# An FP8-rounded feed-forward block behind a long convolution on Trainium2: block 0's convolution pieces, one sum and three queue steps moved

## The chip, the cores and the metric

The kernel runs on one core of one Trainium2 chip. The metric is the device time of one execution in microseconds, as the median of several runs; a kernel's other numbers come from one execution that the hardware profiler recorded.

## What is computed

The input `x` is 128 x 32 x 512 float32: 128 samples, 32 channels, 512 positions. A state-space kernel of 512 taps per channel is computed from small parameters, every channel of `x` is convolved with its own taps (causally), a skip term `D` is added, positions behind a sample's length are set to zero, and the result goes through a gated feed-forward layer whose inputs are rounded to FP8 steps. Its output is added to `x`. Cut to what matters:

```python
def _L0_cond_ref(u, log_dt, C, log_A_real, A_imag, D, length):
    K = _get_kernel(log_dt, C, log_A_real, A_imag, Lq)
    ...
    y = jnp.fft.irfft(uf * kf[None], n=n)[..., :Lq]
    y = y + u * D[:, None]
    mask = (jnp.arange(Lq)[None, :] < length[:, None]).astype(u.dtype)
    return y * mask[:, None, :]

def _L0_ffn_ref(x, gate_w, up_w, down_w, ...):
    gate_out = _fake_quant_fp8_linear(x, gate_w, gate_in_scale, gate_w_scale)
    up_out = _fake_quant_fp8_linear(x, up_w, up_in_scale, up_w_scale)
    hidden = jax.nn.silu(gate_out) * up_out
    return _fake_quant_fp8_linear(hidden, down_w, down_in_scale, down_w_scale)

x = x + _L0_ffn_ref(_L0_cond_ref(x, ..., itok_B_78_3631), ...)
```

## The kernel before

**Tiles.** The 32 channels are cut into 8 blocks of 4; a block is 4 x 128 = 512 tokens. For each block the kernel does four things. TensorE convolves each channel `h` with a Toeplitz matrix of its taps (`conv`, matmuls `y_ps<-xt,toep`, float32, in four pieces called distances 0 to 3, of 512, 384, 256 and 128 columns). ScalarE and VectorE turn the result into rounded inputs `yq`. TensorE then multiplies them with the gate and up weights, in 11 chunks of the hidden size, each chunk 8 matmuls of 512 columns; ScalarE makes the SiLU (`sil<-gate_ps`), VectorE the product (`hv<-up_ps,sil`, function `product`) and the rounding of pairs of chunks (`hc` on ScalarE, `ht`, `hq` and a clip on VectorE). Last, TensorE multiplies `hq` with the down weights (`down_ps<-wd,hq`), ScalarE reads that out, and a DMA of the GpSimd queue adds it to `x` in `out`.

**The chain of one channel of y.** Convolution in `y_ps`; `mask_y` on VectorE (`ym<-y_ps,mask`); `scale_y` (`yv`, two activations) and `magnitude_y` (`yc`, two activations) on ScalarE; `sum_y` (`yt<-yc,yv`), `round_y` (`yq<-yc,yt`) and `clip_y` (`yq<-yq`) on VectorE.

**Order.** Every engine has its own instruction stream, written out by hand, with semaphores between them. A block is 11 slots, one for each chunk `c`. Beside chunk `c` of block `g`, TensorE does four down matmuls of block `g-1` and pieces of convolutions of later blocks, as the table `CONV_PLAN` says: an entry `c: [(step, h, distances)]` puts these pieces of channel `h` of block `g + step` into slot `c`. Channels 0 and most of 1 are done two blocks ahead, the rest one block ahead. VectorE's and ScalarE's work on y is placed by `MASK_PLAN`, `SCALE_PLAN`, `MAGNITUDE_PLAN`, `SUM_PLAN` and `ROUND_PLAN`. The gate matmuls of a chunk wait until the product of the chunk two before is done, since the two chunks share a PSUM bank:

```python
at_least(pe, silu_done, n - 1)
at_least(pe, prod_done, n - 1)
```

**Block 0** has nothing to run beside it yet, so it starts channel by channel: `by_channel(h)` does chunks 0 and 1 for channel `h` alone (128 columns, 16 matmuls), as soon as `clip_y(0, 0, h)` is done, with the convolutions of block 1's channels 0 and 1 between them. Slots 0 and 1 of block 0 then hold only convolution pieces, and slot 2 is the first with 512-column gate matmuls.

**Queues.** The SyncE queue (SP) stores the taps of the last 20 channels to a DRAM scratch when ScalarE has copied them from PSUM (`copy_k(2)`), and loads `xt` and `toep` of the next blocks and copies `x` to `out` (`copy_x`). `next_conv(3, 1)` waits for block 1's four convolutions (`y_ready` of 8), then loads block 3's `xt` and `toep`. The GpSimd queue loads the weights at the start.

In the trace, lines are: 489 `conv`, 515 `by_channel`, 547 gate and up, 503 down, 598 the last down part, 825 `mask_y`, 833 `sum_y`, 844 `round_y`, 851 `clip_y`, 860 `product`, 868, 877 and 885 the rounding of pairs, 362, 363, 370 and 373 `scale_y` and `magnitude_y`, 344 `copy_k`, 381 `hc`, 388 the read-out of down, 398 the SiLU.

Of the kernel before, what the change touches and what calls it, by code (L numbers as in the profile page):

```python
# [32 lines left out]
HB = 4  # L33
# [45 lines left out]
def adaln_ffn_kernel(nc, xT, xn, params, scales, unit, stepped, wg_d, wu_d, wd_d, out):  # L79
# [4 lines left out]
    with ExitStack() as ctx:  # L84
# [97 lines left out]
        def at_least(eng, s, v):  # L182

            if not (isinstance(v, int) and v <= 0):
                eng.wait_ge(s, v)

        def k_in_bank(i, half):

            js = K_GROUPS[i]
            bank, lo = (down_ps, gate_ps, down_ps)[i][half], (0, 0, 2 * KB)[i]  # L190
            return bank[0:KA, lo:lo + (js.stop - js.start) * KB].rearrange("p (j b) -> p j b", b=KB)

        def rows_of_k(i, half):
            return krow[:].rearrange("p (j f) b -> p j f b", f=2)[:, K_GROUPS[i], half]
# [18 lines left out]
        def _(sp):  # L213
# [8 lines left out]
            def load_x_t(g, par):  # L222
                sp.dma_start(xt[par][:], xT[g]).then_inc(xt_in[par], 16)

            def load_toep(g, par):
                sp.dma_start(toep[par][:], toep_d[g]).then_inc(conv_in[par], 16)

            def copy_x(g, par):
                sp.dma_start(out[:, bass.ts(g, HB), :], xn[:, bass.ts(g, HB), :]).then_inc(copied[par], 16)
# [25 lines left out]
            def next_conv(g, par):  # L255
                at_least(sp, y_ready, HB * (g - 1))
                load_x_t(g, par)
                load_toep(g, par)
# [2 lines left out]
            load_x_t(2, 0)  # L261
            sp.wait_ge(k_stored[2], 16)
            load_toep(2, 0)
            copy_x(0, 0)
            next_conv(3, 1)
            copy_x(1, 1)
            with sp.Fori(0, (NBLK - 4) // 2) as j:
                for par in range(2):
# [49 lines left out]
        def _(act):  # L318
# [21 lines left out]
            def copy_k(i):  # L340

                for half in range(2):
                    act.wait_ge(k_ready, 2 * i + half + 1)
                    nc.scalar.copy(rows_of_k(i, half), k_in_bank(i, half)).then_inc(k_copied, 1)
# [67 lines left out]

            act.wait_ge(scales_ready, 1)
            for h in range(HB):
                if h:
                    scale_y(0, h)
                else:
                    cols = slice(0, L // 2)
                    act.wait_ge(ym_first, 1)
                    nc.scalar.activation(yv[0][:, 0, cols], ym[0][:, cols], ACT.Copy,  # L420
                                         scale=fac[:, D_GATE:D_GATE + 1]).then_inc(yv_first, 1)
                    nc.scalar.activation(yv[0][:, 1, cols], ym[0][:, cols], ACT.Copy,
                                         scale=fac[:, D_UP:D_UP + 1]).then_inc(yv_first, 1)
                    act.wait_ge(ym_done, 1)
                magnitude_y(0, h)
            copy_k(2)
            scale_y(1, 0)
            magnitude_y(1, 0)
            slots(0, 0, None, True, 2)
# [10 lines left out]
        def _(pe):  # L440
# [67 lines left out]
            def by_channel(h):  # L508

                pe.wait_ge(yq_ready, h + 1)  # L510
                cols = slice(h * B, (h + 1) * B)
                for c in range(2):
                    for ps, wt, version, ready in ((gate_ps, wg, 0, gate_ready), (up_ps, wu, 1, up_ready)):
                        for k in range(LB):
                            mm = nc.tensor.matmul(ps[c][:, cols], wt[:, k, c * P:(c + 1) * P],
                                                  yq[0][:, version, k, cols], start=(k == 0), stop=(k == LB - 1))
                        if h == HB - 1:
                            mm.then_inc(ready, 1)

            def beside(g, par, half, c, down, ahead):  # L520

                for step, h, distances in CONV_PLAN.get(c, ()):
                    if step <= ahead and (down or (step, h) != (1, 1)):
                        conv(g + step, (par + step) % 2, half + (1 if step == 2 else par), h, distances)
                if down:
                    down_part(g - 1, 1 - par, c)
# [44 lines left out]
            by_channel(1)  # L571
            conv(1, 1, 0, 1, [0, 1, 3, 2])
            by_channel(2)
            by_channel(3)
            pe.wait_ge(middle_in, 32)
            slots(0, 0, 0, False, 2)
# [28 lines left out]
        def _(dve):  # L605
# [222 lines left out]
            def sum_y(g, h):  # L828

                m = HB * g + h  # L830
                q = h % 2
                at_least(dve, yscaled, m + 1)
                v.scalar_tensor_tensor(yt[q][:], yc[q][:], FLOOR, yv[q][:], ALU.max, ALU.add).then_inc(yt_done, 1)  # L833
# [75 lines left out]
            def slots(g, par, ahead, before, plan):  # L909
                first = before is None  # L910
                for c in range(CH):
# [16 lines left out]
                    if c in plan and c < 9 and not (first and c == 3):  # L928
                        rounded(PAIRS * g + plan[c], g, par, plan[c])
                    if ahead and c in SUM_PLAN and not (first and c == 2):  # L930
                        sum_y(g + 1, SUM_PLAN[c])
                    if c - 1 in plan:
# [70 lines left out]

CONV_PLAN = {
# [5 lines left out]
MASK_PLAN = {0: 1, 3: 2, 5: 3}  # L1012
SCALE_PLAN = {0: (1, 0), 1: (1, 1), 4: (1, 2), 6: (1, 3)}
MAGNITUDE_PLAN = {1: (1, 0), 2: (1, 1), 5: (1, 2), 7: (1, 3)}
SUM_PLAN = {2: 0, 3: 1, 6: 2, 8: 3}
ROUND_PLAN = {4: 0, 5: 1, 7: 2, 9: 3}
H_BEHIND = {3: 0, 7: 1, 10: 2}
H_EVEN = {3: 0, 7: 1, 9: 2, 10: 3}
# [60 lines left out]
```

## Time and profile before

| what | us |
|---|---|
| median of 3 runs (325.42 to 325.95) | 325.68 |
| the profiled execution's own time | 325.52 |
| its span, first to last instruction | 323.8 |
| TensorE busy (PE) | 310.2 (96%) |
| VectorE busy (DVE) | 303.2 (94%) |
| ScalarE busy (ACT) | 206.9 (64%) |

The profiled time is 1.72 us longer than the span. The granted TensorE clock is 1.000 of 2.4 GHz in all of it. A line of the timeline is: start in us, duration in us, engine, line of the kernel, operation, output and inputs with shape, count of merged instructions, and in brackets how long the engine sat idle before it and what ended that. TensorE's matmuls are pipelined and their ends are modelled, so a row's duration reaches over the start of the next one: the pace of TensorE is read from one start to the next, and its real gap can be larger than the idle time in the bracket. Some matmul records are missing: a group of four then shows as three.

### The profile page before, as it was taken

The page shows a single profiled execution, that of the slowest core. Times are in us where ns is not written, and L with a number is a line of the kernel's source. Part 1 is how long each engine was busy: PE and PEld are TensorE (multiplying, and loading weights), DVE is VectorE, ACT ScalarE, POOL GpSimd, SP SyncE. Part 2 cuts the span into 40 slices and gives each one's busy share as a digit, 9 for nine tenths or more (in the row PEclk, how much of TensorE's full clock was granted, in tenths as well). Part 3 has the DMA queues.
Part 4 walks back from the last instruction along what each step waited for, and adds up shares of the span by engine and source line. Part 5 has one row for each costly group of instructions (what it writes and reads, how often), then busy time and mean ns, then how long its engine had stood idle before and what let it go on. Part 6 is the DMA issues. An engine that isn't in the chain of part 4 may idle for free.

```text
span 323.8 us, 4771 instructions
## 1 busy us (share of the span) xinstructions
PE 310.2 (96%) x1569; PEld 162.9 (50%) x1595; DVE 303.2 (94%) x464; ACT 206.9 (64%) x318; POOL 12.5 (4%) x20
## 2 busy tenths in 40 slices
PE   1999999999999999999999999999999999989996
PEld 1467554545455554555455454555455454534444
DVE  6999999999999999999998999989998999989784
ACT  4858788188755777486845868376863959364540
POOL 2031000000001000010001000010001000010010
PEclk9999999999999999999999999999999999999999
DMA  6879999300002690078202780067401650051028
GB/s 201 181 181 231 268 278 383 148 1 2 0 0 28 150 343 3 1 130 279 110 0 36 165 317 1 0 121 249 150 0 16 134 243 0 0 97 34 2 31 228
DMA packets 14014, 38.38 MB, mean 119 GB/s; under 512 B 1470, under 2 KB 6558, under 8 KB 11052
## 3 DMA queue, kind: packets, MB, share of 16 engines
q1 hardware_dynamic: 8412, 26.58, 23.2%
q0 software_dynamic: 5584, 11.57, 20.6%
q8 instruction: 10, 0.16, 0.2%
q14 instruction: 8, 0.07, 0.1%
HBM read 33.90 MB, written 15.81 MB: 154 GB/s over the span
## 4 chain that ended last, share of the span: by engine, by line
PE 72%; DVE 19%; issue 4%; ACT 4%; DMA 1%; DVEq 0%; ACTq 0%
PE gate_ps L547 19%; PE up_ps L547 18%; PE down_ps L503 17%; PE y_ps L489 15%; DVE hv L860 3%; DVE yq L844 3%; DVE yt L833 2%; DVE hq L877 2%; DVE ht L868 2%; PE y_ps L598 1%; DVE ym L825 1%; PE down_ps L598 1%; ACT hc L381 1%; DMA prm<-in_params 1%; DVE hq L885 1%
## 5 line engine op out<-in xcount | busy, mean ns | idle before, releaser
L398 ACT ACTIVATE sil<-gate_ps,fac 128x512 f32<-128x512 f32 (+1 forms) x88 | 59.6, 680 | 67.8 <-PE gate_ps L547 66.8
L547 PE MATMUL gate_ps<-yq,wg 128*128 128x512 bf16 (+3 forms) x365 | 88.2, 363 | 2.7 <-DVE hv L860 2.4
L547 PE MATMUL up_ps<-yq,wu 128*128 128x512 bf16 (+3 forms) x367 | 88.4, 363 | 0.3
L489 PE MATMUL y_ps<-xt,toep 128*128 128x512 f32 (+1 forms) x248 | 78.1, 434 | 0.0
L503 PE MATMUL down_ps<-wd,hq 128*128 128x512 bf16 (+1 forms) x295 | 76.8, 379 | 0.7
L860 DVE SCALAR_TENSOR_TENSOR hv<-up_ps,fac,sil 128x512 f32<-128x512 f32 (+1 forms) x88 | 65.5, 744 | 8.2 <-ACT sil L398 6.6
L381 ACT ACTIVATE hc<-hv 128x1024 f32<-128x1024 f32 (+1 forms) x48 | 47.0, 980 | 20.9 <-DVE hq L877 19.8
L547 PEld LDWEIGHTS gate_ps<-yq,wg 128*128 128x128 bf16 x372 | 35.6, 100 | 43.6 <-ACT sil L398 4.0
L489 PEld LDWEIGHTS y_ps<-xt,toep 128*128 128x128 f32 x248 | 45.9, 190 | 19.9 <-issue 2.4
L868 DVE SCALAR_TENSOR_TENSOR ht<-hc,hv 128x1024 f32<-128x1024 f32 (+1 forms) x48 | 54.1, 1127 | 1.9 <-ACT hc L381 1.9
L547 PEld LDWEIGHTS up_ps<-yq,wu 128*128 128x128 bf16 x372 | 36.3, 100 | 38.3
L877 DVE SCALAR_TENSOR_TENSOR hq<-hc,ht 128x1024 bf16<-128x1024 f32 (+1 forms) x48 | 53.8, 1126 | 0.3
L503 PEld LDWEIGHTS down_ps<-wd,hq 128*128 128x128 bf16 (+1 forms) x308 | 30.1, 98 | 37.9 <-issue 12.6
L844 DVE SCALAR_TENSOR_TENSOR yq<-yc,yt 128x1024 bf16<-128x1024 f32 x32 | 39.0, 1217 | 0.1
L833 DVE SCALAR_TENSOR_TENSOR yt<-yc,yv 128x1024 f32<-128x1024 f32 x31 | 37.7, 1217 | 0.0
L370 ACT ACTIVATE yc<-ym,fac 128x512 f32<-128x512 f32 x32 | 22.8, 713 | 2.9 <-DVE yq L844 2.9
L362 ACT ACTIVATE yv<-ym,fac 128x512 f32<-128x512 f32 x31 | 22.1, 712 | 3.2 <-DVE ym L825 3.2
L373 ACT ACTIVATE yc<-ym,fac 128x512 f32<-128x512 f32 x32 | 22.8, 712 | 0.0
L363 ACT ACTIVATE yv<-ym,fac 128x512 f32<-128x512 f32 x31 | 22.0, 709 | 0.0
L825 DVE TENSOR_TENSOR ym<-y_ps,mask 128x512 f32<-128x512 f32 x31 | 21.1, 681 | 0.0
L388 ACT ACTIVATE res<-down_ps,fac 128x512 f32<-128x512 f32 x28 | 19.0, 679 | 2.2 <-PE down_ps L503 2.1
L885 DVE TENSOR_SCALAR hq<-hq 128x1024 bf16<-128x1024 bf16 (+1 forms) x48 | 18.4, 397 | 0.3
(155 smaller groups left out, 118.1 us busy)
## 6 DMA issues: line engine op xcount, KB each, us to landing
xt<-in_xT SPq DMA_DIRECT2D x8, 1024.0 KB, 7.6
out<-in_x SPq DMA_DIRECT2D x7, 1024.0 KB, 5.6
out<-res POOLq DMA_DIRECT2D x7, 1024.0 KB, 7.8
toep<-kpad_scratch SPq DMA_DIRECT2D x6, 1024.0 KB, 10.0
toep<-kpad_scratch SPq DMA_DIRECT2D x8, 256.0 KB, 3.9
wd<-in_down POOLq DMA_DIRECT2D x1, 1280.0 KB, 21.3
xt<-in_x SPq DMA_DIRECT2D x1, 1024.0 KB, 7.3
out<-xt SPq DMA_DIRECT2D x3, 256.0 KB, 3.1
```

The source lines that it names most:

```text
L370: gate = nc.scalar.activation(yc[q][:, 0, :], ym[q][:], ACT.Abs, scale=fac[:, R_GATE:R_GATE + 1])
L381: nc.scalar.activation(hc[e % 2][0:w, 0:k], hv[e % 2][0:w, 0:k], ACT.Abs, scale=UP20).then_inc(abs_ready, 1)
L398: nc.scalar.activation(sil[b][0:w, :], gate_ps[b][0:w, :], ACT.Silu, scale=fac[0:w, S_GATE:S_GATE + 1]).then_inc(silu_done, 1)
L489: last = nc.tensor.matmul(y_ps[h % 2][:, d * P:L], toep[par][:, h, d * P:(d + 1) * P], xt[par][:, h, 0:L - d * P], start=(d == 0), stop=(d ...
L503: mm = nc.tensor.matmul(down_ps[t % 2][:], hq[par][0:w, k, t * P:(t + 1) * P], wd[0:w, k, :], start=(k == 0), stop=(k == CH - 1))
L547: mm = nc.tensor.matmul(ps[b][0:w, cols], wt[:, k, c * P:c * P + w], yq[par][:, version, k, cols], start=(k == 0), stop=(k == LB - 1))
L825: v.tensor_tensor(ym[q][:], y_ps[q][:], mask[:].rearrange("p k b -> p (k b)"), ALU.mult).then_inc(ym_done, 1)
L833: v.scalar_tensor_tensor(yt[q][:], yc[q][:], FLOOR, yv[q][:], ALU.max, ALU.add).then_inc(yt_done, 1)
L844: v.scalar_tensor_tensor(yq_of(par, h), yc[q][:].rearrange("p v (k b) -> p (v k) b", k=LB), FLOOR, yt[q][:].rearrange("p v (k b) -> p (v k ...
L860: v.scalar_tensor_tensor(hv[c // 2 % 2][0:w, c % 2], up_ps[b][0:w, :], fac[0:w, S_UP:S_UP + 1], sil[b][0:w, :], ALU.mult, ALU.mult).then_i ...
L868: v.scalar_tensor_tensor(ht[e % 2][0:w, 0:k], hc[e % 2][0:w, 0:k], FLOOR, hv[e % 2][0:w, 0:k], ALU.max, ALU.add).then_inc(t_done, 1)
L877: v.scalar_tensor_tensor(hq[par][0:w, 2 * e:2 * e + k, :], hc[e % 2][0:w, 0:k], FLOOR, ht[e % 2][0:w, 0:k], ALU.max, ALU.subtract, reverse ...
```

## The change

Five edits:

1. In front of `by_channel(3)`, TensorE does the first piece (distance 0, 512 columns) of channel 2 of block 1.
2. In block 0 a table of its own, `FIRST_PLAN`, takes the place of `CONV_PLAN`; every piece there comes one slot earlier.
3. `SUM_PLAN` has 9 in place of 8 for channel 3, in all blocks that have a block behind them: `sum_y` of the fourth channel comes behind the product of chunk 9 (the tenth) and right in front of its own `round_y`.
4. `copy_k(2)` on ScalarE comes ahead of `scale_y(0, 3)` in place of behind `magnitude_y(0, 3)`.
5. On the SyncE queue `next_conv(3, 1)` comes ahead of `copy_x(0, 0)`.

```diff
@@ -261,8 +261,8 @@
             load_toep(2, 0)
+            next_conv(3, 1)
             copy_x(0, 0)
-            next_conv(3, 1)
             copy_x(1, 1)
@@ -412,6 +412,8 @@
             for h in range(HB):
+                if h == HB - 1:
+                    copy_k(2)
                 if h:
                     scale_y(0, h)
@@ -423,7 +425,6 @@
                 magnitude_y(0, h)
-            copy_k(2)
             scale_y(1, 0)
@@ -519,8 +520,8 @@
-                for step, h, distances in CONV_PLAN.get(c, ()):
-                    if step <= ahead and (down or (step, h) != (1, 1)):
+                for step, h, distances in (CONV_PLAN if down else FIRST_PLAN).get(c, ()):
+                    if step <= ahead:
@@ -571,6 +572,7 @@
             by_channel(2)
+            conv(1, 1, 0, 2, [0])
             by_channel(3)
@@ -1003,6 +1005,10 @@
+FIRST_PLAN = {
+    6: [(2, 0, [0])], 7: [(2, 0, [1, 3])], 8: [(2, 0, [2]), (2, 1, [0])], 9: [(2, 1, [1, 3])],
+    1: [(1, 2, [1, 3])], 2: [(1, 2, [2]), (1, 3, [0])], 3: [(1, 3, [1, 3])], 4: [(1, 3, [2])],
+}
 CONV_PLAN = {
     7: [(2, 0, [0])], 8: [(2, 0, [1, 3])], 9: [(2, 0, [2]), (2, 1, [0])], 10: [(2, 1, [1, 3])],
@@ -1012,7 +1018,7 @@
-SUM_PLAN = {2: 0, 3: 1, 6: 2, 8: 3}
+SUM_PLAN = {2: 0, 3: 1, 6: 2, 9: 3}
```

**TensorE, from the end of the third channel's `by_channel` to slot 3 of block 0.** Before:

```order
L515 MATMUL up_ps<-yq,wu 128x128 x4
L515 MATMUL gate_ps<-yq,wg 128x128 x4
L515 MATMUL up_ps<-yq,wu 128x128 x4
L515 MATMUL gate_ps<-yq,wg 128x128 x4
L515 MATMUL up_ps<-yq,wu 128x128 x4
L489 MATMUL y_ps<-xt,toep 128x512
L547 MATMUL gate_ps<-yq,wg 128x512 x4
L547 MATMUL up_ps<-yq,wu 128x512 x4
L489 MATMUL y_ps<-xt,toep 128x384
L489 MATMUL y_ps<-xt,toep 128x128
```

and now:

```order
L516 MATMUL up_ps<-yq,wu 128x128 x4
L490 MATMUL y_ps<-xt,toep 128x512
L516 MATMUL gate_ps<-yq,wg 128x128 x4
L516 MATMUL up_ps<-yq,wu 128x128 x4
L516 MATMUL gate_ps<-yq,wg 128x128 x4
L516 MATMUL up_ps<-yq,wu 128x128 x4
L490 MATMUL y_ps<-xt,toep 128x384
L490 MATMUL y_ps<-xt,toep 128x128
L548 MATMUL gate_ps<-yq,wg 128x512 x4
L548 MATMUL up_ps<-yq,wu 128x512 x4
```

The 512-column piece went from behind the fourth channel's 16 matmuls to ahead of them, and the 384 and 128 columns from behind the first 512-column chunk to ahead of it.

**VectorE, slots 8 to 10 of block 0** (a number behind a name is the buffer; `hv` is the product, `yt` the sum, `yq` the rounding and then the clip). Before:

```order
L860 SCALAR_TENSOR_TENSOR hv0<-up_ps0,fac,sil0 128x512
L868 SCALAR_TENSOR_TENSOR ht1<-hc1,hv1 128x1024
L833 SCALAR_TENSOR_TENSOR yt1<-yc1,yv1 128x1024
L885 TENSOR_SCALAR hq0<-hq0 128x1024
L860 SCALAR_TENSOR_TENSOR hv0<-up_ps1,fac,sil1 128x512
L844 SCALAR_TENSOR_TENSOR yq1<-yc1,yt1 128x8x128
L851 TENSOR_SCALAR yq1<-yq1 128x8x128
L860 SCALAR_TENSOR_TENSOR hv1<-up_ps0,fac,sil0 96x512
```

and now:

```order
L862 SCALAR_TENSOR_TENSOR hv0<-up_ps0,fac,sil0 128x512
L870 SCALAR_TENSOR_TENSOR ht1<-hc1,hv1 128x1024
L887 TENSOR_SCALAR hq0<-hq0 128x1024
L862 SCALAR_TENSOR_TENSOR hv0<-up_ps1,fac,sil1 128x512
L835 SCALAR_TENSOR_TENSOR yt1<-yc1,yv1 128x1024
L846 SCALAR_TENSOR_TENSOR yq1<-yc1,yt1 128x8x128
L853 TENSOR_SCALAR yq1<-yq1 128x8x128
L862 SCALAR_TENSOR_TENSOR hv1<-up_ps0,fac,sil0 96x512
```

The sum `yt1` left the place two ahead of the tenth product and now stands directly in front of the rounding that reads it; the number of instructions is the same.

## Rows read from the trace of the kernel before

**Rows 1.** Busy time by stretch: slots 2 to 10 of block 0, block 1, block 2.
```profile
core 0: us, PE busy (x) PEld busy (x) DVE busy (x) ACT busy (x) POOL busy (x), PEclk, DMA share, GB/s
...
36.80:61.40 24.60, 23.62 (x100) 12.18 (x100) 24.43 (x31) 17.34 (x26) 0.00 (x0) 1.00 1.02 317
61.40:98.94 37.54, 37.27 (x168) 19.10 (x173) 36.90 (x48) 24.08 (x36) 0.00 (x0) 1.00 0.00 1
98.94:136.09 37.15, 36.99 (x170) 19.30 (x172) 36.61 (x48) 25.39 (x38) 0.90 (x1) 1.00 0.40 114
```
**Rows 2.** Timeline of TensorE around the fourth channel and slot 2 of block 0.
```profile
34.93 0.39 PE L515 MATMUL up_ps<-yq,wu 128*128 128x128 bf16 x4
35.59 0.40 PE L515 MATMUL gate_ps<-yq,wg 128*128 128x128 bf16 x4 [0.27 <-DVE yq L851]
...
36.49 1.08 PE L489 MATMUL y_ps<-xt,toep 128*128 128x512 f32 x2
37.93 0.81 PE L547 MATMUL gate_ps<-yq,wg 128*128 128x512 bf16 x3 [0.36 <-DVE hv L860]
```
**Rows 3.** Timeline of VectorE, the same stretch, then slots 8 to 10.
```profile
35.45 1.22 DVE L833 SCALAR_TENSOR_TENSOR yt<-yc,yv 128x1024 f32<-128x1024 f32 x1
36.82 0.75 DVE L860 SCALAR_TENSOR_TENSOR hv<-up_ps,fac,sil 128x512 f32<-128x512 f32 x1
...
58.97 1.22 DVE L833 SCALAR_TENSOR_TENSOR yt<-yc,yv 128x1024 f32<-128x1024 f32 x1
60.11 0.42 DVE L885 TENSOR_SCALAR hq<-hq 128x1024 bf16<-128x1024 bf16 x1
60.45 0.74 DVE L860 SCALAR_TENSOR_TENSOR hv<-up_ps,fac,sil 128x512 f32<-128x512 f32 x1
61.11 1.21 DVE L844 SCALAR_TENSOR_TENSOR yq<-yc,yt 128x1024 bf16<-128x1024 f32 x1
```
**Rows 4.** Timeline of TensorE, first gate matmuls of slots 0, 2, 3, 7, block 1.
```profile
61.43 0.82 PE L547 MATMUL gate_ps<-yq,wg 128*128 128x384 bf16 x4 [0.60 <-DVE hv L860]
...
68.03 1.02 PE L547 MATMUL gate_ps<-yq,wg 128*128 128x512 bf16 x4
...
71.55 1.02 PE L547 MATMUL gate_ps<-yq,wg 128*128 128x512 bf16 x4
...
84.70 1.02 PE L547 MATMUL gate_ps<-yq,wg 128*128 128x512 bf16 x4
```
**Rows 5.** Timeline of VectorE, products of block 1 that those gates wait for.
```profile
67.13 0.75 DVE L860 SCALAR_TENSOR_TENSOR hv<-up_ps,fac,sil 128x512 f32<-128x512 f32 x1
...
70.66 0.75 DVE L860 SCALAR_TENSOR_TENSOR hv<-up_ps,fac,sil 128x512 f32<-128x512 f32 x1
...
83.80 0.75 DVE L860 SCALAR_TENSOR_TENSOR hv<-up_ps,fac,sil 128x512 f32<-128x512 f32 x1
```
**Rows 6.** Timeline of VectorE, one sum followed by its own rounding.
```profile
29.14 1.22 DVE L833 SCALAR_TENSOR_TENSOR yt<-yc,yv 128x1024 f32<-128x1024 f32 x1
30.39 1.23 DVE L844 SCALAR_TENSOR_TENSOR yq<-yc,yt 128x1024 bf16<-128x1024 f32 x1
```
**Rows 7.** Timelines of VectorE and TensorE, blocks 6 and 7, the stretch's first and last.
```profile
264.10 1.23 DVE L868 SCALAR_TENSOR_TENSOR ht<-hc,hv 128x1024 f32<-128x1024 f32 x1
...
292.20 0.74 DVE L860 SCALAR_TENSOR_TENSOR hv<-up_ps,fac,sil 128x512 f32<-128x512 f32 x1
...
293.08 1.02 PE L547 MATMUL gate_ps<-yq,wg 128*128 128x512 bf16 x4 [0.22 <-DVE hv L860]
```
**Rows 8.** Timeline of ScalarE around `copy_k(2)`.
```profile
28.92 0.72 ACT L362 ACTIVATE yv<-ym,fac 128x512 f32<-128x512 f32 x1 [0.77 <-DVE ym L825]
...
31.39 0.71 ACT L344 COPY hq<-down_ps 16x320 f32<-16x320 f32 x2
```
**Rows 9.** DMA issues: block 2's Toeplitz load at 39.36; the small down-weight load.
```profile
toep<-kpad_scratch SPq DMA_DIRECT2D x1, 1024.0 KB, 9.8
...
wd<-in_down POOLq DMA_DIRECT2D x1, 96.0 KB, 26.2
```

## The prediction, written before the changed kernel ran

> **What bounds the kernel now.** I read the busy time by stretch first. From slot 2 of block 0 to the end of block 1 both TensorE and VectorE are nearly full: VectorE 24.43 of 24.60 us in block 0 and 36.90 of 37.54 in block 1, TensorE 23.62 and 37.27 [rows 1]. From block 2 on TensorE needs 37.15 us a block, with 36.99 busy, and the same 37.15 returns in blocks 3 to 5, so TensorE is the bound there. Block 1 is 0.39 us longer than block 2 for the same work. So the question is which of the two engines is late at the end of block 0, and that needs the timelines.
>
> A gate group of TensorE starts right behind the product of the chunk two before, where that product is late. The product of chunk 0 of block 1 starts at 67.13 and takes 0.75, the gate of slot 2 starts at 68.03, 0.15 behind its end; the products at 70.66 and 83.80 stand the same way to the gates at 71.55 and 84.70 [rows 4, 5]. So TensorE follows VectorE up to 84.70 us, and the idle times of 0.27, 0.36 and 0.60 us before it in block 0 [rows 2, 4] are what it has in hand over VectorE. VectorE meanwhile works back to back: from its first product at 36.82 [rows 3] to 65.1 us its timeline has no idle row, then one of 0.26 us, which is a loop through VectorE's own results (its rounding lets ScalarE make `hc`, which lets VectorE go on). A delay of VectorE at 36.8 us is therefore carried to 84.70, and TensorE, full from there, to the end.
>
> **The change, part by part.**
>
> *The first piece ahead of the fourth channel.* TensorE ends the third channel at about 35.15 (four starts of 0.056 us from 34.93) and waits until 35.59 for the fourth channel's `yq` [rows 2], a gap of 0.44 us by starts. The piece is 512 columns in float32: its two records are followed by the next work 0.86 us after the first in every slot where TensorE doesn't wait. It fills the 0.44 and pushes the fourth channel back by 0.42: to 36.01. Behind that channel hang the first SiLU and the first product of VectorE. VectorE is ready for it: the sum before it starts at 35.45 and the next instruction could follow 1.13 us later, at 36.58, yet the product starts at 36.82 [rows 3], when the SiLU is there. So the product goes to 37.24, and **VectorE loses 0.42 us**. The bounds: nothing, if the product waited for something else; 0.50 if the change of float32 to bf16 matmuls costs a little more. I take 0.42.
>
> *The rest of the pieces one slot earlier.* This is 0.86 us of TensorE work taken from behind slot 2's gate and put ahead of it, where TensorE waits for the product anyway (before, idle 0.36 at 37.93 [rows 2]). The total is unchanged. With it TensorE runs from slot 2 at 38.1 to slot 10, which ends at about 60.2 (22.96 us before, less 0.86). That leaves it 0.5 to 0.9 us ahead of each product. Cost nothing, gain nothing, since VectorE is the one that is late. If VectorE weren't full, this would be worth the gap of 0.44.
>
> *The fourth sum behind the tenth product.* In block 0 the tenth product now comes one sum earlier: from 60.45 back by 1.14 (58.97 to 60.11 [rows 3]) and on by the 0.42, to 59.73. The gate of block 1's slot 0, which waits 0.60 us for it [rows 4], can start at about 60.7 instead of 61.43. But the stall doesn't vanish, it moves. The sum and its rounding now follow each other: such a pair is 1.25 us apart [rows 6], against 1.14 for a sum followed by an instruction that doesn't read it [rows 3]. So **VectorE loses 0.11 us more**, the fourth `yq` is ready at 63.3, where TensorE now asks for it, and the product of chunk 0 of block 1 moves from 67.13 by 0.42 + 0.11 to 67.66. The gate at 68.03 then starts at 68.56. What is late next is that product: TensorE comes a good 1 us too early for it and waits.
>
> A rule speaks against this 0.11. The Trainium skill (VectorE: DVE Perf Modes, The DRAIN you can't avoid) says that the next VectorE instruction can't start until the pipeline is empty and that a semaphore between two costs nothing extra. By it the term would be 0 and the sum 0.42. The rows show 1.25 against 1.14, and I go by them.
>
> *In blocks 1 to 5* the same pair costs 0.11 in VectorE each time, but VectorE has slack there (36.61 busy of 37.15 in block 2 [rows 1]; from block 2 on it waits 0.6 to 1.3 us a block for a SiLU in slot 0): nothing. *In block 6* it is different: TensorE has less to do beside it, and VectorE runs back to back from 264.10, with one idle of 0.72 that again is the loop through its own roundings, to the product at 292.20, which the gate at 293.08 waits for [rows 7]. So the last 0.11 us count once more. Bounds 0 and 0.12.
>
> *`copy_k(2)` earlier.* Its two copies are 0.71 us and come into an idle 0.77 of ScalarE that ends at 28.92 [rows 8]. Their sources are ready at about 28.1, so `scale_y(0, 3)` is late by 0.1 at most; its result is used by VectorE only at 32.59, 1.1 us after it is there. Nothing. On the SyncE queue the store and the loads of block 2's `xt` and `toep` come up to 3.2 us earlier.
>
> *`next_conv(3, 1)` ahead of `copy_x(0, 0)`.* Block 1's last convolution ends at about 45.9, so block 3's loads go out 2 us earlier and `copy_x(0, 0)` 6 us later than 39.8. The copy is wanted by ScalarE only at block 1's slot 5 (some 77 us). Block 2's Toeplitz load took 9.8 us from 39.36 [rows 9], to 49.2; its first piece was due at 51.52 and is now due at 49.4. Issued at 36 to 39 with no copy beside it, it lands in time. The cover is thin only if none of the 3.2 us comes through.
>
> **The sum.** 0.42 + 0.11 + 0.11 = 0.64 us. The profiled execution took 325.52, so 326.16 by it; the median of the runs is 0.16 above the profiled one, and I add to the median: 325.68 + 0.65 = **326.3**.
>
> **The rivals.**
>
> *Faster: TensorE is the real bound.* If VectorE has slack that the timeline hides, the three idle times of TensorE, 0.27 + 0.36 + 0.60 = 1.23 us [rows 2, 4], are what can be won, and the time is 324.5. For it speaks that TensorE has the highest busy share. Against it, the three gates of block 1 at exactly 0.15 us behind their products. It decides if the product at 67.13 comes earlier than now. The Trainium skill (Perfetto Trace Analysis, Optimization Strategies) would have it so: keep the matmul engine as highly used as possible. Chance 0.13.
>
> *No change: the delay of the first product is smaller or partly absorbed.* The product waits 0.24 us now; if part of the 0.42 hides in waits that I read as back to back, 0.0 to 0.3 us are left, 325.9. Chance 0.20.
>
> *Slower by more: a transfer becomes late.* If block 2's Toeplitz load lands where it did, 49.2, or up to 1.5 us later because `xt` and the weights share the engines with it, or if the small down-weight load (31.3 + 26.2 = 57.5 [rows 9]), wanted at 60.7, is pushed back by more than 4 us, TensorE stalls until VectorE runs dry: 1 us on top of the sum, 327.3. Chance 0.07.
>
> *The change doesn't do what it says* for the queue steps: the store lands when it did, since the DMA engines are full; this costs nothing and changes no number.
>
> The forecast itself has 0.60.
>
> **How the numbers follow.** Two tenths of a per cent, 0.65 us, is about what a measurement of this kernel can tell from no change, and the forecast sits on that line: I give 0.33 of its 0.60 to slower and 0.27 to the same. Slower is 0.33 + 0.07 = 0.40, the same 0.27 + 0.20 = 0.47, faster 0.13. The range reaches from 325.1, below the unchanged case, to 327.0, the forecast with both bounds and the runs' spread; outside are most of the faster case and most of the late transfer.
>
> **What would show it.** Right: the fourth channel's first gate at 36.0, the first product at 37.2; the gate of block 1 at about 60.7, with no long wait; then a wait before the gate of slot 2, which starts near 68.6; block 2 starting near 99.5 (98.94 before); sum to rounding 1.25 apart in every block. Wrong: the first product still at 36.8, or block 2 starting at or below 98.9, or an idle row of TensorE in front of a `y_ps` piece at 49 us.

## The result and the profile after

The changed kernel takes 326.39 us (median of 17 runs, 326.12 to 327.55), the kernel before 325.61 us beside it (17 runs, 325.42 to 326.16). The ratio is 1.0027, 95% interval 1.0021 to 1.0034, so it is slower by more than 0.2%. The profiled execution took 326.39 against 325.52, its span 324.7 against 323.8, with the granted clock at 1.000 of 2.4 GHz again. TensorE's busy time is unchanged at 310.2 us; VectorE's is 303.8 in place of 303.2.

Line numbers of the kernels below are 0 to 10 above those of before, by the lines added. The busy time by stretch of the changed kernel, with the stretches moved by about their shift (+0.6 at slot 2, +0.74 at block 2), answers to [rows 1]:

```profile
core 0: us, PE busy (x) PEld busy (x) DVE busy (x) ACT busy (x) POOL busy (x), PEclk, DMA share, GB/s
37.40:62.00 24.60, 23.88 (x105) 12.58 (x106) 24.37 (x31) 17.27 (x26) 0.00 (x0) 1.00 1.00 296
61.60:99.68 38.08, 36.91 (x165) 18.52 (x168) 37.38 (x49) 24.10 (x36) 0.00 (x0) 1.00 0.00 1
99.68:136.83 37.15, 36.99 (x170) 19.30 (x172) 36.58 (x47) 25.05 (x38) 0.90 (x1) 1.00 0.40 114
```

VectorE is as full as before, and TensorE idles 1.17 of 38.08 us in the second stretch, where it idled 0.27 of 37.54 before: it got ahead and waits. Block 2 takes 37.15 us again.

TensorE's timeline, which answers to [rows 2, 4, 7]:

```profile
35.32 1.08 PE L490 MATMUL y_ps<-xt,toep 128*128 128x512 f32 x2
36.24 0.39 PE L516 MATMUL gate_ps<-yq,wg 128*128 128x128 bf16 x4
...
37.13 1.08 PE L490 MATMUL y_ps<-xt,toep 128*128 128x384 f32 x4
38.56 0.81 PE L548 MATMUL gate_ps<-yq,wg 128*128 128x512 bf16 x3 [0.34 <-DVE hv L862]
...
60.91 0.82 PE L548 MATMUL gate_ps<-yq,wg 128*128 128x384 bf16 x4 [0.33 <-DVE hv L862]
...
68.76 1.02 PE L548 MATMUL gate_ps<-yq,wg 128*128 128x512 bf16 x4 [0.81 <-DVE hv L862]
...
85.44 1.02 PE L548 MATMUL gate_ps<-yq,wg 128*128 128x512 bf16 x4
...
293.95 1.02 PE L548 MATMUL gate_ps<-yq,wg 128*128 128x512 bf16 x4 [0.22 <-DVE hv L862]
```

Block 1 starts 0.52 us earlier than before (61.43, now 60.91), and all of it is given back before slot 2's gate, most of it in a wait of 0.81 us that was not there. From there to block 6 every gate is 0.74 us late (68.03 to 68.76 is 0.73, 84.70 to 85.44), and at block 7 0.87 (293.08 to 293.95).

VectorE's timeline, which answers to [rows 3, 5]:

```profile
35.60 1.22 DVE L835 SCALAR_TENSOR_TENSOR yt<-yc,yv 128x1024 f32<-128x1024 f32 x1
37.45 0.75 DVE L862 SCALAR_TENSOR_TENSOR hv<-up_ps,fac,sil 128x512 f32<-128x512 f32 x1 [0.63 <-ACT sil L398]
...
59.93 0.74 DVE L862 SCALAR_TENSOR_TENSOR hv<-up_ps,fac,sil 128x512 f32<-128x512 f32 x1
60.59 1.21 DVE L835 SCALAR_TENSOR_TENSOR yt<-yc,yv 128x1024 f32<-128x1024 f32 x1
61.84 1.23 DVE L846 SCALAR_TENSOR_TENSOR yq<-yc,yt 128x1024 bf16<-128x1024 f32 x1
63.10 0.43 DVE L853 TENSOR_SCALAR yq<-yq 128x1024 bf16<-128x1024 bf16 x1
...
67.87 0.75 DVE L862 SCALAR_TENSOR_TENSOR hv<-up_ps,fac,sil 128x512 f32<-128x512 f32 x1
```

Before, the product came 1.37 us behind the sum (35.45, 36.82), now 1.85 (35.60, 37.45): 0.48 us lost. The tenth product is at 59.93, which is 60.45 - 1.14 + 0.63, the shift that it started with and one sum less. Sum and rounding are 1.25 apart (60.59, 61.84), rounding and clip 1.26 (61.84, 63.10). The product of chunk 0 of block 1 is 0.74 late. So the 0.87 of the profiled executions is:

| part | us | read from |
|---|---|---|
| all of the start is late | 0.15 | sum of the fourth channel, 35.45 to 35.60 |
| first product, behind that sum | 0.48 | 1.37 to 1.85 |
| sum in front of its own rounding, block 0 | 0.11 | 0.74 at 67.87, less 0.63 at 37.45 |
| the same, block 6 | 0.13 | 0.87 at 293.95, less 0.74 |

The first row is in none of the edits. Block 0's first convolution starts 0.17 us later than before, when its Toeplitz load has landed (issued at 14.36 before and 14.30 now, ahead of everything that the edits move), and VectorE's fourth sum comes 17.68 and 17.66 us behind that start. The start in the kernel before and in the changed one:

```profile
17.77 0.92 PE L560 MATMUL y_ps<-xt,toep 128*128 128x256 f32 x4
```

```profile
17.94 0.92 PE L561 MATMUL y_ps<-xt,toep 128*128 128x256 f32 x4 [0.35 <-DMA toep<-kpad_scratch]
```

### The profile page after: what moved, and what is told of

It is laid out like the page before. It is cut to its first block, busy times and chain, and to the rows that moved or that the text cites. A ratio compares the mean times of both kernels' runs of the same rounds, so it can differ in the third digit from the quotient of the medians.

```text
span 324.7 us, 4771 instructions
## 1 busy us (share of the span) xinstructions
PE 310.2 (96%) x1569; PEld 162.5 (50%) x1595; DVE 303.8 (94%) x464; ACT 206.6 (64%) x318; POOL 12.5 (4%) x20
## 4 chain that ended last, share of the span: by engine, by line
PE 76%; DVE 16%; issue 4%; DMA 2%; ACT 1%; DVEq 0%; ACTq 0%; SPq 0%
PE y_ps L490 19%; PE gate_ps L548 18%; PE up_ps L548 17%; PE down_ps L504 17%; DVE hv L862 3%; DVE yq L846 3%; DVE hq L879 2%; DVE ht L870 2%; DVE yt L835 2%; PE y_ps L600 1%; DMA toep<-kpad_scratch 1%; PE down_ps L600 1%; ACT hc L381 1%; DVE hq L887 1%; DMA prm<-in_params 1%
```

## The experiments

Each ran in 5 rounds against the kernel before, whose median was 325.64, 325.55, 325.62 and 325.61 in the four groups of runs (e1 to e4; e5 to e8; e9, e10; e11, e12). Theory A is the account that the prediction gives, with the first term as measured. A rival stands with its letter in the expectation that names it.

### e1: the pieces alone

```diff
+            conv(1, 1, 0, 2, [0])
             by_channel(3)
-                for step, h, distances in CONV_PLAN.get(c, ()):
+                for step, h, distances in (CONV_PLAN if down else FIRST_PLAN).get(c, ()):
```

> The kernel before with edits 1 and 2 alone: the piece ahead of the fourth channel and the table FIRST_PLAN. Theory A (VectorE's chain sets the time from block 0 to 84.7 us, and the piece delays its first product): the first product of VectorE starts 1.85 us behind the sum before it (1.37 in the kernel before), block 2 starts 0.48 us later, the time is 0.48 us longer (ratio 1.0015). Theory B (TensorE's gaps are what counts, and the loss comes from the moved sum or the queues): the gap of 0.44 us is filled, the time is 0 to 0.44 us shorter (ratio 0.9987 to 1.0000).

Measured: 326.04 us, ratio 1.0014 (1.0005 to 1.0023). Its VectorE and TensorE timelines:

```profile
35.49 1.22 DVE L834 SCALAR_TENSOR_TENSOR yt<-yc,yv 128x1024 f32<-128x1024 f32 x1
37.14 0.75 DVE L861 SCALAR_TENSOR_TENSOR hv<-up_ps,fac,sil 128x512 f32<-128x512 f32 x1 [0.43 <-ACT sil L398]
```

```profile
35.01 1.08 PE L489 MATMUL y_ps<-xt,toep 128*128 128x512 f32 x2
35.92 0.39 PE L515 MATMUL gate_ps<-yq,wg 128*128 128x128 bf16 x4
...
61.75 0.82 PE L547 MATMUL gate_ps<-yq,wg 128*128 128x384 bf16 x4 [1.46 <-DVE hv L861]
```

The product comes 1.65 behind its sum, so 0.28 is lost and not 0.48. The piece explains it: it starts where the third channel ends, at 35.01 here and at 35.32 in the changed kernel, and the product follows the piece by 2.13 us in both (37.14, 37.45). The loss is the end of the third channel plus 2.13, against the sum plus 1.37; TensorE was 0.31 earlier in this execution and VectorE 0.11, and the difference of 0.20 is that between the two losses. The term depends on how the engines happen to stand to each other, and that is set at the first convolution: it starts at 17.94 in the changed kernel and at 17.62 here, TensorE's piece is 17.4 us behind it in both, but the sum is 17.66 behind it there and 17.87 here. In all six executions where that convolution started at 17.77 or later, the sum came 17.66 to 17.68 behind it; where it started earlier, VectorE did not follow in full (17.71 us and more). The other half of the account holds too: without the moved sum, TensorE waits 1.46 us at block 1's first gate, its lead of one slot and no gain.

### e2: the sum alone

```diff
-SUM_PLAN = {2: 0, 3: 1, 6: 2, 8: 3}
+SUM_PLAN = {2: 0, 3: 1, 6: 2, 9: 3}
```

> The kernel before with edit 3 alone: the fourth sum behind the tenth product in all blocks. Theory A: the gate of block 1 no longer waits (it starts at 60.7 in place of 61.4, idle 0), but the gate of slot 2 of block 1 starts 0.12 us later (68.15), block 2 too (99.06), and a second 0.12 comes in at block 7 (the gate that was at 293.08 comes at 293.32); the time is 0.24 us longer (ratio 1.0007). Theory B: the stall of 0.60 us that goes away is a gain, the time is up to 0.6 us shorter (ratio 0.9982).

Measured: 325.97 us, ratio 1.0017 (1.0008 to 1.0026). Its VectorE and TensorE timelines:

```profile
60.19 1.22 DVE L833 SCALAR_TENSOR_TENSOR yt<-yc,yv 128x1024 f32<-128x1024 f32 x1
61.44 1.23 DVE L844 SCALAR_TENSOR_TENSOR yq<-yc,yt 128x1024 bf16<-128x1024 f32 x1
```

```profile
60.89 0.81 PE L547 MATMUL gate_ps<-yq,wg 128*128 128x384 bf16 x4
...
68.36 1.02 PE L547 MATMUL gate_ps<-yq,wg 128*128 128x512 bf16 x4 [0.81 <-DVE hv L860]
```

The wait of 0.60 ahead of block 1 [rows 4] is gone and stands at slot 2 with 0.81 us: the stall moved and grew. That gate is 0.33 later than before, of which 0.21 is the start (fourth sum at 35.66 where it was 35.45), so 0.12 belongs to the pair, and another 0.12 to 0.14 is in the gate at 293.55, behind block 6. These executions show that the start moves by itself: nothing that the fourth sum waits for is changed in e1, e2 and e5 to e8, and it stood at 35.49, 35.66, 35.46, 35.42, 35.40 and 35.70 (in e8 the clip ahead of it alone took 0.69 us, in the kernel before 0.43).

### e3: the queue steps alone

```diff
+            next_conv(3, 1)
             copy_x(0, 0)
-            next_conv(3, 1)
+                if h == HB - 1:
+                    copy_k(2)
-            copy_k(2)
```

> The kernel before with edits 4 and 5 alone: the tap copies and their store sooner, block 3's loads ahead of the first copy of x. Theory A: no time in it, ratio 1.0000 within 0.0003. The store on the SyncE queue goes out 3 us sooner (29 in place of 32), the Toeplitz load 2 to 3 us sooner. Theory C (the part of the loss that the VectorE chain does not explain, some 0.15 us that the changed kernel's timeline already shows at 34 us, comes from ScalarE's new order or the transfers): 0.15 us longer, ratio 1.0005, and the clip of the fourth channel starts at 35.26 in place of 35.10.

Measured: 325.56 us, ratio 1.0001 (0.9992 to 1.0009). The fourth sum is at 35.45 and block 2 starts at 98.95 (before 35.45 and 98.94): the queue steps cost nothing, and theory C falls: the 0.15 us do not come from them. The ScalarE timeline, which answers to [rows 8]:

```profile
28.06 0.73 ACT L344 COPY hq<-down_ps 16x320 f32<-16x320 f32 x2
28.93 0.72 ACT L362 ACTIVATE yv<-ym,fac 128x512 f32<-128x512 f32 x1
```

The copies fit into the idle time, and the scale step starts at 28.93 where it was 28.92. (In the changed kernel it starts at 29.09, but there the mask step that it reads is 0.17 us later too, by the start.) One thing is new in this profile, though: block 2 takes 37.44 us (98.95 to 136.39). Its TensorE timeline, SyncE timeline and DMA issues:

```profile
122.72 1.03 PE L548 MATMUL up_ps<-yq,wu 128*128 128x512 bf16 x4
123.77 1.12 PE L490 MATMUL y_ps<-xt,toep 128*128 128x512 f32 x2
```

```profile
112.50 0.41 SPq L226 DMA_DIRECT2D toep<-kpad_scratch  x1
```

```profile
toep<-kpad_scratch SPq DMA_DIRECT2D x1, 1024.0 KB, 11.0
```

The first piece of block 4 is due 0.86 behind the up matmuls, at 123.58, and starts at 123.77; its Toeplitz load was issued at 112.50 and took 11.0 us, to 123.5. This load had hardly any time in hand; the row does not name what the piece waited for. e11 tests it.

### e4: the 512 columns back behind the fourth channel

```diff
@@ the changed kernel
-            conv(1, 1, 0, 2, [0])
             by_channel(3)
-    1: [(1, 2, [1, 3])], 2: [(1, 2, [2]), (1, 3, [0])], ...
+    0: [(1, 2, [0])], 1: [(1, 2, [1, 3])], 2: [(1, 2, [2]), (1, 3, [0])], ...
```

> The changed kernel with edit 1 undone: the 512-column piece stands behind the fourth channel again, so that slots 0 and 1 of block 0 do the pieces of 512, 384 and 128 columns in a row, all else as changed. Theory A: the first product is on time again (1.37 us behind the sum before it), and 0.48 us come back: 0.24 us longer than the kernel before (ratio 1.0007), 0.5 to 0.6 shorter than the changed kernel. TensorE reaches slot 2 at about 37.8 and starts there 0.1 to 0.2 us later than before, at most 0.1 us of which could reach the time. Theory B: the time stays at that of the changed kernel, 0.88 us longer.

Measured: 326.24 us, ratio 1.0023 (1.0011 to 1.0036). **This missed**: the product is on time again and the time hardly came back. VectorE's, TensorE's and ScalarE's timelines:

```profile
35.61 1.22 DVE L834 SCALAR_TENSOR_TENSOR yt<-yc,yv 128x1024 f32<-128x1024 f32 x1
36.98 0.75 DVE L861 SCALAR_TENSOR_TENSOR hv<-up_ps,fac,sil 128x512 f32<-128x512 f32 x1
...
48.57 0.75 DVE L861 SCALAR_TENSOR_TENSOR hv<-up_ps,fac,sil 128x512 f32<-128x512 f32 x1 [0.23 <-ACT sil L398]
...
67.82 0.75 DVE L861 SCALAR_TENSOR_TENSOR hv<-up_ps,fac,sil 128x512 f32<-128x512 f32 x1
```

```profile
36.66 1.94 PE L490 MATMUL y_ps<-xt,toep 128*128 128x512 f32 x6
38.65 0.81 PE L548 MATMUL gate_ps<-yq,wg 128*128 128x512 bf16 x3
```

```profile
45.11 0.69 ACT L398 ACTIVATE sil<-gate_ps,fac 128x512 f32<-128x512 f32 x1 [1.91 <-PE gate_ps L548]
...
47.87 0.67 ACT L398 ACTIVATE sil<-gate_ps,fac 128x512 f32<-128x512 f32 x1
```

The product is 1.37 behind its sum. But now both slots' pieces stand between the fourth channel and slot 2, and its gate starts at 38.65, 0.72 later than before (37.93) where the start moved by 0.16. TensorE is then late for the next slots, ScalarE's SiLU starts at 45.11 and the one after it, behind its other work, at 47.87 (before 44.38 and 47.14), and VectorE's product waits for that at 48.57. The product of block 1 is 0.69 late. Of the 0.69, 0.16 is the start and 0.11 the pair of the moved sum, so 0.42 came this way. As these rows read, TensorE has in block 0 only the 0.36 us ahead of slot 2 [rows 2] in hand over the products, less than a piece, and what exceeds it comes back through ScalarE. The pieces one slot earlier are free in the changed kernel only because the first of them went ahead of the fourth channel, and there it costs 0.48. This way of the 0.42 is read from one trace; no run has the pieces in this order without the moved sum.

### e5 and e6: the sum moved in blocks 1 to 5, and in block 6

```diff
@@ the kernel before, with sums in place of SUM_PLAN
+                    sums = {2: 0, 3: 1, 6: 2, 9 if 0 < g < 6 else 8: 3}
```

e6 has `9 if g == 6 else 8` there.

> The kernel before with the fourth sum behind the tenth product in blocks 1 to 5 alone. Theory A (the pair of a sum and its own rounding costs VectorE 0.12 us, and that reaches the time only where VectorE is the late engine): VectorE shows 1.25 us from sum to rounding in these five blocks, its wait for a SiLU in slot 0 gets shorter by the same, blocks 2 to 6 start when they did (98.94, 136.09, 173.24, 210.39, 247.54, behind a shift of up to 0.2 of the start), and the time is unchanged, ratio 1.0000. Theory D (each such pair costs its 0.12 us wherever it stands): five times 0.12, 0.6 us longer, ratio 1.0018.

> The kernel before with the fourth sum behind the tenth product in block 6 alone. Theory A: everything up to block 7 is unchanged, the last gate of block 7 that waits for VectorE (293.08) comes 0.12 us later, the time is 0.12 us longer, ratio 1.0004, which the clock alone can hardly tell from 1; the trace decides. If VectorE had slack there: no shift at all.

Measured: e5 325.80 us, ratio 1.0005 (0.9996 to 1.0013); e6 325.69, ratio 1.0006 (0.9997 to 1.0016). Medians can't tell 0.1 us from nothing here, but the traces can. In e5 the blocks start at 98.96, 136.11, 173.26, 210.41 and 247.56, 37.15 apart to the hundredth, block 7's gate is at 293.10 where it was 293.08 [rows 7], and its execution took 325.54: the pair is hidden in the middle blocks, and the 1.0018 of theory D lies outside the interval. In e6 the start was 0.03 early, sum and rounding of block 6 are 1.25 apart (279.10, 280.35), and that gate is at 293.18: 0.13 net. As the prediction had it.

### e7: each clip of y behind the next product

```diff
@@ the kernel before
                     product(n, m, par, c)
+                    if ahead and c - 1 in ROUND_PLAN and not (first and c == 5):
+                        clip_y(g + 1, 1 - par, ROUND_PLAN[c - 1])
                         round_y(g + 1, 1 - par, ROUND_PLAN[c])
-                        clip_y(g + 1, 1 - par, ROUND_PLAN[c])
```

The change made a dependent pair; this takes one apart. The clip reads what the rounding just wrote; here a product stands between them.

> The kernel before, with the clip of each y moved from right behind its rounding to behind the next product, in all blocks: the same instructions, but no clip follows the rounding that it reads. Theory A says that this gives VectorE 0.11 us a pair: 3 pairs in block 0 and 1 in block 1 before the product at 83.8, and 4 in block 6. So block 2 starts 0.44 us sooner (98.50), and a second 0.44 us comes before the gate that was at 293.08; the time is 0.8 to 0.9 us shorter, ratio 0.9973 to 0.9976. Theory E, that two dependent instructions cost VectorE nothing extra: the time is unchanged; the clip of the fourth y comes 0.7 us later, and if TensorE waits for it, 0.1 us longer. The Trainium skill (VectorE: DVE Perf Modes, The DRAIN you can't avoid) states what theory E says: a semaphore between two VectorE instructions costs nothing extra.

Measured: 324.86 us, ratio 0.9977 (0.9969 to 0.9986), the first kernel here that is clearly faster. Its VectorE timeline, TensorE timeline and waits of VectorE (us in total, times, longest):

```profile
60.81 1.21 DVE L844 SCALAR_TENSOR_TENSOR yq<-yc,yt 128x1024 bf16<-128x1024 f32 x1
61.94 0.74 DVE L860 SCALAR_TENSOR_TENSOR hv<-up_ps,fac,sil 96x512 f32<-96x512 f32 x1
62.60 0.41 DVE L851 TENSOR_SCALAR yq<-yq 128x1024 bf16<-128x1024 bf16 x1
...
269.24 0.75 DVE L860 SCALAR_TENSOR_TENSOR hv<-up_ps,fac,sil 128x512 f32<-128x512 f32 x1 [0.19 <-ACT sil L398]
```

```profile
61.13 0.82 PE L547 MATMUL gate_ps<-yq,wg 128*128 128x384 bf16 x4 [0.44 <-DVE hv L860]
...
67.63 1.03 PE L547 MATMUL gate_ps<-yq,wg 128*128 128x512 bf16 x4
```

```profile
DVE hv L860 <- ACT sil L398: 8.8, 15, 1.0
```

From the rounding to what follows it is 1.13 us (60.81, 61.94), against 1.26 from a rounding to its own clip, shown above for the changed kernel. Slot 2's gate comes at 67.63 for 68.03, block 2 at 98.33 for 98.94. From the first product to that of chunk 0 of block 1, with three pairs taken apart between, it is 29.94 us (36.76, 66.70) for 30.31: 0.12 a pair. A dependent pair costs 0.11 to 0.13 us of VectorE, and where VectorE is the late engine, that is time.

The total is a little less than was expected, 0.69 us by the medians, and it is not spread as was expected. Block 2 is 0.56 us early net of the start (0.05), in place of 0.44: the product that the gate at 84.70 waited for passes its clip too (it is 0.87 us earlier, 82.93 for 83.80), and TensorE no longer waits there. The gate that was at 293.08 comes at 292.39, only 0.08 more: in block 6 VectorE now waits for a SiLU at 269.24, where it ran back to back, so most of what it saves there goes into that wait. Over the whole execution it waits 8.8 us for SiLUs, in 15 places, before 6.6 in 7. Part of e7's gain is thus the product's new place and not the pairs; the 0.12 above is free of that.

In this kernel every instruction that reads the one ahead also waits for the semaphore that the one ahead raises, so no run tells whether the read or that wait costs the 0.12. The rule of the Trainium skill (VectorE: DVE Perf Modes, The DRAIN you can't avoid), by which the pair would have cost nothing extra, does not hold for these pairs (1.26 against 1.13 us); the measurement decides.

### e8: and in slot 1 the sum ahead of the clips

```diff
@@ e7, slot 1
-                    clip(last - 2, 1 - par, PAIRS - 3)
-                    clip(last - 1, 1 - par, PAIRS - 2)
                     rounded_sum(last, PAIRS - 1)
+                    clip(last - 2, 1 - par, PAIRS - 3)
                     rounded(last, g - 1, 1 - par, PAIRS - 1)
+                    clip(last - 1, 1 - par, PAIRS - 2)
                     clip(last, 1 - par, PAIRS - 1)
```

> As the run before it, and in slot 1 of every block the five instructions on the last pairs (two clips, then a sum, a rounding and a clip that each read the one before) are put in the order sum, clip, rounding, clip, clip. Theory A: the sum-rounding and rounding-clip stalls of this short chain (0.05 and 0.06 us) go, 0.1 us at block 1 and 0.1 us at block 7; 0.2 us shorter than the run before it, ratio 0.9967 to 0.9970. Theory E: no difference. If TensorE has become the late engine by then, as it may where its own work is back to back, less than 0.2 us.

Measured: 324.72 us, ratio 0.9971 (0.9960 to 0.9982), the lowest of all, but no clear gain over e7, whose interval it overlaps, and less than the 0.2 us that were expected. In its profile nothing is won at block 2 (98.62, with the fourth sum at 35.70; 0.57 early net of the start, e7 0.56); the gate behind block 6 is at 292.44, 0.89 early net of the start, e7 0.64. It beats the kernel before by 0.8 to 0.9 us and the changed one by 1.7.

### e9: the changed kernel with e7's clips

> The changed kernel with the clips moved as in the run of the clips (each clip of y behind the next product). Theory A: the delays and the savings of VectorE in block 0 simply add, so the first product is again 1.85 us behind the sum before it, and block 2 starts 0.55 to 0.6 us sooner than in the changed kernel, which is where the kernel before has it, within 0.1 us (98.9 to 99.2, behind a shift of the start of up to 0.3); the time is 0.7 to 0.9 us shorter than the changed kernel's, ratio to the kernel before 0.9998 to 1.0006. If the piece ahead of the fourth channel had been hidden by a faster VectorE after all, the time would be that of the clips alone, ratio 0.9977.

The edit is that of e7, made to the changed kernel. Measured: 325.71 us, ratio 0.9996 (0.9987 to 1.0005), a hair below what was expected. In its profile the first product is 1.84 behind the sum (35.46, 37.30) as in the changed kernel, and block 2 starts at 98.98 for 99.68, which is 0.56 us net of the start. The gain and the loss add up, since both are VectorE's. Block 2 again takes 0.40 too much (98.98 to 136.53), with the same piece late.

### e10: only half of the piece ahead

```diff
@@ the kernel before: 256 columns of the 512, the other 256 behind the fourth channel
+            half_piece(0)
             by_channel(3)
```

If the full piece costs because it is larger than the gap of 0.44 us, half of it should fit.

> The kernel before, with only half of the 512-column piece (256 columns, 0.43 us of TensorE) ahead of the fourth channel, the other half where the whole piece stood; FIRST_PLAN and the other edits are not in it. Theory A (what counts is how far the piece sticks out of the gap of 0.44 us): the half fits, the first product stays 1.37 us behind the sum (at most 1.43), nothing after it moves, and the time is unchanged, ratio 1.0000 within 0.0004. If what costs is that anything at all stands between the third and the fourth channel (a change of operand type, another weight load), the product is late by 0.1 us or more and the time follows it, ratio 1.0003 or more. If TensorE's earlier arrival at slot 2 were worth something, ratio below 0.999.

Measured: 325.53 us, ratio 0.9999 (0.9990 to 1.0008). Its TensorE and VectorE timelines:

```profile
34.99 0.65 PE L525 MATMUL y_ps<-xt,toep 128*128 128x256 f32 x2
35.50 0.40 PE L515 MATMUL gate_ps<-yq,wg 128*128 128x128 bf16 x4
...
37.84 0.81 PE L556 MATMUL gate_ps<-yq,wg 128*128 128x512 bf16 x3 [0.78 <-DVE hv L870]
```

```profile
35.36 1.22 DVE L843 SCALAR_TENSOR_TENSOR yt<-yc,yv 128x1024 f32<-128x1024 f32 x1
36.73 0.75 DVE L870 SCALAR_TENSOR_TENSOR hv<-up_ps,fac,sil 128x512 f32<-128x512 f32 x1
```

It fits: 1.37 behind the sum, nothing lost, although work of another type stands between the two channels. And nothing is won: TensorE's wait for the product, 0.36 before, is 0.78. Work put into a gap of an engine that isn't late makes its next gap longer.

### e11 and e12: the Toeplitz loads ahead of the copy in the SyncE loop

```diff
@@ e3, and e8 for e12
+                    next_conv(2 * j + 4 + par, par)
                     at_least(sp, added[par], 16 * (j + 1))
                     copy_x(2 * j + 2 + par, par)
-                    next_conv(2 * j + 4 + par, par)
```

> The queue edits (4 and 5) plus one more in the SyncE loop: the loads of xt and toep of block g + 4 go ahead of the wait for the sum of block g and of copy_x, so block 4's Toeplitz load, which lands 0 to 1.6 us before its first piece needs it, should be issued near 82 us and not at 112. Theory F (a load that comes just in time caused the one-off of 0.3 and 0.4 us in block 2 of two profiled executions): block 2 takes 37.15 in this profile, the piece near 123.6 starts without delay; the median is that of the kernel before or up to 0.1 us less, ratio 0.9990 to 1.0005. Rival G (a disturbance of another kind, not the load): the one-off has no tie to the load, and comes or not as before. Rival H (the earlier loads now run beside other transfers): a wait elsewhere, 0.2 us or more slower.

> The fastest kernel so far (the clips of y behind the next product, and in slot 1 the sum ahead of the two clips; 324.72 us) with the same step in the SyncE loop. The kernel of the later clips issued the block 4 load at 111.39, landed 121.7 and used it at 123.24: 1.5 us in hand. Theory F: nothing to win in the median, ratio to the kernel before 0.9965 to 0.9975. Rival H: above 0.9980.

Measured: e11 325.66 us, ratio 1.0003 (0.9994 to 1.0012); e12 324.74, ratio 0.9968 (0.9958 to 0.9978), no better than e8. The SyncE and TensorE timelines of e11:

```profile
81.91 0.39 SPq L226 DMA_DIRECT2D toep<-kpad_scratch  x1
```

```profile
123.55 1.02 PE L490 MATMUL y_ps<-xt,toep 128*128 128x512 f32 x2
```

The load is issued 30 us earlier, the piece is on time, and block 2 takes 37.15 (98.92 to 136.07). In the profiled executions of the other ten experiments and both kernels the load was issued between 111.32 and 113.02 (111.87 before, 113.02 after), and took 9.9 to 11.5 us. In e3 it landed at 123.50 with its piece due at 123.58, in e9 at 123.7 (112.20 + 11.5) with the piece due at 123.61, and these two pieces were 0.2 and 0.3 late; in all the others it landed 0.4 us or more ahead, e10 with 11.1 us from 111.96 among them, and no piece was late. That fits a load just in time (theory F). H, that the earlier load hurts elsewhere, is excluded by e12, whose interval ends below the 0.9980 set for it; e11's interval alone leaves room for 0.2 us. A profile without the delay is no proof by itself, since most executions had none, and the medians don't move. How many of the timed runs it touched stays open.

## Why the prediction was right, point by point

**The verdict and the size.** 326.3 forecast, 326.39 measured, inside the range, and slower as the account said, though 0.47 was given to the same and 0.40 to slower: the forecast lay on the line between them, and the interval (1.0021 to 1.0034) lies just above it.

**The bound.** That VectorE was the late engine from slot 2 of block 0 to block 1 is right. Every loss on it was carried to 84.70 and on (0.73, 0.74, 0.74), e7's relief of it came through, and TensorE's waits moved without being worth anything. The rival of a bound TensorE falls: its full lead in e1 ended as one wait of 1.46 us.

**The first piece.** The mechanism was right, the term was mis-sized: 0.42 predicted, 0.48 in the profile of the changed kernel and 0.28 in that of e1. The prediction took 0.86 for the piece and the change of kind; the fourth channel starts 0.92 behind it (35.32 to 36.24; 0.91 in e1, 35.01 to 35.92), which is the 0.06 between 0.42 and 0.48. It also took the stand of the two engines from one execution, and that stand moves by some 0.2 us with the start of the first convolution. The upper bound of 0.50 held. That 0.42 lies between the two measured values is in part luck.

**The other pieces one slot earlier.** "Cost nothing" holds for the whole change, but the reason given was short of one condition: e4 showed that they cost 0.4 us or so by another way, TensorE, ScalarE's SiLU, VectorE, as soon as the first piece is not ahead of the fourth channel. The cover was VectorE's own delay, which the prediction did not name as such.

**The sum in front of its rounding.** 0.11 predicted and 0.11 measured in block 0 (0.12 in e2), 0.11 and 0.13 in block 6, nothing in blocks 1 to 5 (e5). The gate at block 1 came at 60.91 (0.15 of it the start) where 60.7 was forecast, and the wait moved to slot 2's gate, 68.76 for 68.56.

**The queue steps.** Nothing (e3), with the loads of block 2 issued at 29.45 and 36.93 in the changed kernel and not late. The late transfer of the rival list does exist, but in block 2 and for block 4's load, a place the prediction did not look at.

**The sum of the terms.** 0.64 predicted; the traces give 0.48 + 0.11 + 0.13 = 0.72, the medians 0.78 and the ratio 0.88. e1 and e2 add +0.40 and +0.33 in their medians. The 0.15 us by which the start was late in the profiled execution is in no edit and comes with the landing of the first Toeplitz load; whether that load lands later in the changed kernel as a rule, and how much of it is in the medians, 0.06 to 0.16 by these figures, was not settled.

## What to carry to other kernels

Before filling an engine's gap, ask which engine is late there: if it is another one, filled gaps only come back as longer waits (0.36 to 0.78 us in e10), and a piece longer than the gap costs the difference at once. On a full VectorE, put an instruction that reads something else between a writer and its reader; that was worth 0.12 us a pair here, and moving the clips of y so made the kernel 0.7 us faster with no work removed (e7), until ScalarE's SiLU became what VectorE waited for. Where two orders of work cover each other's delays, undo them one at a time in both directions before calling one of them free.

## What the runs showed of the hardware that was not expected

- A VectorE instruction on 128x1024 elements is followed after 1.13 to 1.15 us by one that doesn't read its result, and after 1.24 to 1.26 by one that does, where neither waits for another engine; each reader also waits here for the semaphore of the one ahead.
- A 512-column float32 piece ahead of bf16 matmuls takes 0.91 or 0.92 us, start to start, in front of 128-column matmuls of the y chain, where 0.86 was read in the slots. The change of type alone is not the reason: the pieces in the slots stand in front of bf16 matmuls too, of 512 columns (51.52 to 52.38 in the kernel before).
- Kernels with the same instructions up to the fourth channel's sum had it at 35.40 to 35.70 us from execution to execution, and the end of TensorE's third channel moved against it by 0.2 us. Most of it goes back to the first convolution, which started between 17.61 and 17.99 in the fourteen profiled executions, in four of the six latest after a wait for its Toeplitz load. A difference of 0.2 us between two profiled executions needs a place where it arises before it is put down to an edit.
- The same 1 MB Toeplitz load took 9.9 to 11.5 us in the same place of the program; with 10.8 to 11.9 us between its issue and its first use, that spread decided whether block 2 took 0.3 to 0.4 us more.
